# Expert tiles of a gated cross-attention network: rows as two planes of 16-bit halves, fetched by transposing transfers

## What is computed

```python
diff = x[:, :, None, :] - keys
dist2 = jnp.sum(diff * diff, axis=-1)
logits = -dist2 + jnp.einsum('bld,ed->ble', x, rw) + rb
topv, topi = jax.lax.top_k(logits, TOP_K)
w = jax.nn.softmax(topv, axis=-1)
hidden = jax.nn.gelu(jnp.einsum('bld,efd->blef', x, w1) + b1, approximate=False)
exp_out = jnp.einsum('blef,edf->bled', hidden, w2) + b2
sel = jnp.take_along_axis(exp_out, topi[..., None], axis=2)
fused = jnp.sum(w[..., None] * sel, axis=2)
```

## Time and profile before

| | |
|---|---|
| median of 3 runs | 1582.33 us (1581.99 to 1583.48) |
| the profiled execution | 1586.09 us, of which the profile's span is 1584.2 us |
| mean granted clock of PE | 0.963 |
| dispatch beside A3 | about 853 to 1255 us of the span |
| expert loop | 1263 to 1548 us, 144 tiles |
| loading back, mixing, storing | 1549 to 1584 us |
| PE busy | 87% of the span |

### The profile page before, as it was taken

One profiled execution on the slowest core, in us unless ns is written; L12 is line 12 of the kernel. 1 busy time (PEld: TensorE's weight loads), 2 busy tenths in 40 slices (PEclk: granted clock), 3 DMA queues, 4 the chain that ended last, 5 costly groups with the idle time before them and its releaser, 6 DMA issues.

```text
span 1584.2 us, 34370 instructions
## 1 busy us (share of the span) xinstructions
PE 1383.6 (87%) x9959; PEld 1030.9 (65%) x9982; DVE 1103.3 (70%) x3531; ACT 1014.4 (64%) x2931; POOL 534.7 (34%) x631
## 2 busy tenths in 40 slices
PE   4788887998899988998999999999986299999994
PEld 3566665676744465443666666666665199999994
DVE  4788877687777667883666876776665466666665
ACT  2688887554555564225788777777764377777762
POOL 3353467222211411010003242242144455555550
PEclk9999999999999999999999999999987599999998
DMA  8000059500499910000000010010034122222227
GB/s 195 24 8 7 14 84 177 80 0 14 91 177 176 149 34 21 1 0 7 1 8 25 12 34 23 13 35 16 23 125 160 40 65 62 66 65 65 62 57 265
DMA packets 143406, 98.23 MB, mean 62 GB/s; under 512 B 20595, under 2 KB 132510, under 8 KB 142150
## 3 DMA queue, kind: packets, MB, share of 16 engines
q1 hardware_dynamic: 134598, 80.08, 25.4%
q0 software_dynamic: 8704, 16.87, 3.2%
HBM read 43.03 MB, written 54.93 MB: 62 GB/s over the span
## 4 chain that ended last, share of the span: by engine, by line
PE 59%; ACT 13%; DVE 12%; issue 10%; DMA 2%; another core or an unknown queue 1%; SPq 1%; DVEq 1%; POOL 0%; ACTq 0%; POOLq 0%
PE bank L1448 7%; PE bank L1006 7%; PE bank L1440 7%; PE bank L1292 4%; PE bank L1022 4%; ACT arena L1481 4%; PE bank L947 3%; PE bank L1057 3%; ACT att L1618 3%; PE bank L1010 2%; PE bank L1042 2%; PE bank L1032 2%; ACT att L1483 2%; PE bank L929 2%; PE bank L1368 2%
## 5 line engine op out<-in xcount | busy, mean ns | idle before, releaser
L1481 ACT ACTIVATE arena<-bank 128x512 f32<-128x512 f32 (+7 forms) x380 | 245.5, 674 | 151.4 <-PE bank L1355 54.1
L1898 ACT ACTIVATE att<-bank,arena 128x128 f32<-128x128 f32 x576 | 164.5, 371 | 67.5 <-PE bank L1440 64.6
L820 POOL DMA_INDIRECT expert_outputs<-arena x144 | 146.9, 1020 | 146.3 <-issue 99.5
L1618 ACT ACTIVATE att<-bank,arena 128x128 f32<-128x128 f32 x512 | 180.2, 393 | 16.1 <-DVE arena L2156 15.0
L774 POOL DMA_INDIRECT dispatched_rows<-arena x112 | 113.4, 1012 | 177.1 <-DVE arena L2045 116.1
L608 POOL TENSOR_TENSOR ve<-mv,eps 128x4 f32<-128x4 f32 x64 | 12.8, 200 | 423.9 <-DVE mv L1961 414.9
L1448 PE MATMUL bank<-arena,att 128*128 128x128 f32 x1152 | 153.7, 276 | 2.3 <-ACT att L1898 1.1
L1440 PE MATMUL bank<-xnT,arena 128*128 128x128 f32 x1152 | 153.8, 277 | 0.9 <-ACT xnT L1481 0.9
L1448 PEld LDWEIGHTS bank<-arena,att 128*128 128x128 f32 x1152 | 140.1, 192 | 4.8 <-ACT att L1898 4.6
L1440 PEld LDWEIGHTS bank<-xnT,arena 128*128 128x128 f32 x1152 | 141.4, 193 | 1.5 <-ACT xnT L1481 1.5
L1481 ACT ACTIVATE xnT<-bank 128x128 f32<-128x128 f32 (+1 forms) x180 | 63.4, 352 | 90.1 <-PE bank L841 42.4
(11 more groups left out here) (375 smaller groups left out, 3243.6 us busy)
## 6 DMA issues: line engine op xcount, KB each, us to landing
dispatched_rows<-padf SPq DMA_DIRECT2D x16, 2128.5 KB, 32.7
arena<-dispatched_rows SPq DMA_DIRECT2D x144, 64.5 KB
cxT<-in_ctx SPq DMA_DIRECT2D x32, 256.0 KB
arena<-in_L_ffn_w SPq DMA_DIRECT2D x8, 1024.0 KB
arena<-expert_outputs SPq DMA_DIRECT2D x8, 1024.0 KB, 14.3
expert_outputs<-arena POOLq DMA_INDIRECT x144
out_x<-x SPq DMA_DIRECT2D x8, 256.0 KB, 4.2
dispatched_rows<-arena POOLq DMA_INDIRECT x112
```

The lines of the kernel that those rows point to most:

```text
L820: pl.indirect_dma_start(sent_out, bass.IndirectOffsetOnAxis(xtu3[:, s, P:P + 1], 0), yt3[:, s, :], None, bounds_check=TOP3 * TOKENS - 1, o ...
L1481: copy = lambda o, i: nc.scalar.activation(o, i, ACT.Copy)
L1618: last = nc.scalar.activation(ex3_of(w, side)[:, i, :], bank[side][:, i * P:i * P + P], ACT.Exp, bias=nm3[:, w % 2, h:h + 1], accum_out=su ...
L1898: last = nc.scalar.activation(h3[:, s % 2, k * P:k * P + P], bank[s % 2][:, k * P:k * P + P], ACT.Gelu, bias=b1c3[:, s % 4, k:k + 1])
```

## The change

Rows go out as two planes of 16 bits: all 128 low halves of a row's words, then all 128 high halves, then the tag's word. A row keeps its 516 bytes.

- In dispatch ACT's row copy becomes two (`row_halves`), each of as many elements as the one before, but of 16 bits, reading every second half-word. The second, u = 11, stands one step later, ahead of the exponential u = 10.
- In the loop SP fetches a tile by one transposing transfer (128 rows x 256 half-words into 128 partitions x two planes) and one small transfer of the 128 tags (4 bytes each). It reads the places of four tiles at once, in the loop ahead of the wait for the scatter.
- PE's `tile_T` is gone. ACT's copy from PSUM becomes `tile_join`: it waits for the group's transfers, reads the two planes from SBUF and writes low and high half of each word side by side into `xnT`, 256 half-words per partition, in the place in ACT's order where the copy stood.
- POOL takes the tags from a tile of their own.

```diff
-            def load_tile(i, s):
-                at = sp.value_load(tab3[0:1, 1, bass.ds(i, 1)], min_val=0, max_val=UNUSED)
-                sp.dma_start(xt3[:, s, :], sent[bass.ds(at, P), :]).then_inc(sem(f"F3_tiles_loaded{s // GROUP3}"), 16)
-
-            for s in range(SLOTS3):
-                load_tile(s, s)
+            def places_of(i):
+
+                _, places = nc.values_load_multi_w_load_instructions(tab3[0:1, 1, bass.ds(i, GROUP3)], [mybir.EngineType.SP], min_val=0, max_val=UNUSED)
+                return places
+
+            def load_tile(at, s):
+                sp.dma_start_transpose(xth3[:, s, :, :], sent[bass.ds(at, P), 0:HALF_WORDS3]).then_inc(sem(f"F3_tiles_loaded{s // GROUP3}"), 16)
+                sp.dma_start(tagh3[:, s, :], sent[bass.ds(at, P), HALF_WORDS3:2 * ROW3]).then_inc(sem(f"F3_tiles_loaded{s // GROUP3}"), 16)
+
+            for q in range(SLOTS3 // GROUP3):
+                places = places_of(q * GROUP3)
+                for k in range(GROUP3):
+                    load_tile(places[k], q * GROUP3 + k)
             with sp.Fori(1, GROUPS3) as g:
-                for s in range(SLOTS3):
-                    if s % GROUP3 == 0:
-
-                        sp.wait_ge(sem(f"F3_scattered{s // GROUP3}"), g * (16 * GROUP3))
-                    load_tile(g * SLOTS3 + s, s)
+                for q in range(SLOTS3 // GROUP3):
+                    places = places_of(g * SLOTS3 + q * GROUP3)
+                    sp.wait_ge(sem(f"F3_scattered{q}"), g * (16 * GROUP3))
+                    for k in range(GROUP3):
+                        load_tile(places[k], q * GROUP3 + k)
...
-            def tile_T(turn, s):
-                pe.wait_ge(sem(f"F3_tiles_loaded{s % SLOTS3 // GROUP3}"), turn * (16 * GROUP3) + 16 * GROUP3)
-                nc.tensor.transpose(bank[6 + s % 2][:, 0:P], xt3[:, s % SLOTS3, 0:P], ident[:, :]).then_inc(sem("F3_tile_T"), 1)
...
             with pe.Fori(0, GROUPS3 - 1) as g:
                 for s in range(SLOTS3):
-                    tile_T(g + (s + 2) // SLOTS3, s + 2)
                     up(g * SLOTS3 + (s + 1), s + 1)
                     down(g * SLOTS3 + s, s)
...
+            def row_halves(half, h):
+
+                js = ALL if half is None else HALVES[half]
+                n, of = len(js), slice(js[0], js[-1] + 1)
+                return copy(rows_of(half)[0][:, qs_of(js), h * P:h * P + P].rearrange("p (j k) d -> p j k d", j=n),
+                            xrh3[:, of, :, h].unsqueeze(2).to_broadcast([P, n, TOP3, P]))
...
-                    copy(rows_of(half)[0][:, qs_of(js), 0:P].rearrange("p (j k) d -> p j k d", j=n),
-                         xr3[:, of, :].unsqueeze(2).to_broadcast([P, n, TOP3, P])).then_inc(sem("F3_rows_copied"), 1)
+                    row_halves(half, 0)
+                if u == 11:
+                    row_halves(half, 1).then_inc(sem("F3_rows_copied"), 1)
...
-                        if live and not first and more and w in (3, 5, 6):
-                            routing(c - 1, {3: 8, 5: 9, 6: 10}[w])
+                        if live and not first and more:
+                            for u in {3: (8,), 5: (9,), 6: (11, 10)}.get(w, ()):
+                                routing(c - 1, u)
...
-            def tile_T(n, s):
-                act.wait_ge(sem("F3_tile_T"), n + 1)
-                copy(xnT[:, (s % 4) * P:(s % 4) * P + P], bank[6 + s % 2][:, 0:P]).then_inc(sem("F3_tile_xT"), 1)
+            def tile_join(n, turn, s):
+                act.wait_ge(sem(f"F3_tiles_loaded{s % SLOTS3 // GROUP3}"), turn * (32 * GROUP3) + 32 * GROUP3)
+                copy(xnh[:, s % 4, :, :], xth3[:, s % SLOTS3, :, :].rearrange("p h t -> p t h")).then_inc(sem("F3_tile_xT"), 1)
```

More of the change, by code:

```diff
@@ L8 @@
 U32 = mybir.dt.uint32
+U16 = mybir.dt.uint16
 I32 = mybir.dt.int32
@@ L45 @@
 ROW3 = P + 1
+HALF_WORDS3 = 2 * P
 UNUSED = E3 * REGION
@@ L220, in flamingo @@
         padu3 = padf3[:, :].bitcast(U32)
+        padh3 = padf3[:, :].bitcast(U16)
         iota3 = sb("iota3", [E3, NT])
@@ L346, in flamingo @@
         rowsu3 = arena[:, used[0] - SC * ROW3:used[0]].bitcast(U32).rearrange("p (q d) -> p q d", q=SC)
+        rowsh3 = arena[:, used[0] - SC * ROW3:used[0]].bitcast(U16).rearrange("p (q d) -> p q d", q=SC)
         lg3 = ar([P, CB, E3])
@@ L357, in flamingo @@
         xr3 = tmp2
+        xrh3 = tmp2[:, :, :].rearrange("p j d -> p (j d)").bitcast(U16).rearrange("p (j d h) -> p j d h", j=CB, h=2)
+        xnh = xnT[:, :].bitcast(U16).rearrange("p (s t h) -> p s t h", s=4, h=2)
         xrT3 = we2[:, 0:W]
@@ L369, in flamingo @@
         tabf3, tab3 = ar([1, 2, NT]), ar([1, 2, NT], I32)
+        at = used[0] = -(-used[0] // 8) * 8
+        xt3 = ar([P, SLOTS3, P])
+        xth3 = arena[:, at:used[0]].bitcast(U16).rearrange("p (s h t) -> p s h t", s=SLOTS3, h=2)
         at = used[0]
-        xt3 = ar([P, SLOTS3, ROW3])
-        xtu3 = arena[:, at:used[0]].bitcast(U32).rearrange("p (s d) -> p s d", s=SLOTS3)
+        tag3 = ar([P, SLOTS3])
+        tagu3, tagh3 = arena[:, at:used[0]].bitcast(U32), arena[:, at:used[0]].bitcast(U16).rearrange("p (s h) -> p s h", s=SLOTS3)
         yt3 = ar([P, SLOTS3, P])
@@ L390, in rows_of @@
         def rows_of(half):
-            return (rows3, rowsu3, di3) if half is None else (last3, lastu3, lastdi3)
+            return (rowsh3, rowsu3, di3) if half is None else (lasth3, lastu3, lastdi3)
         def qs_of(js):
@@ L402, in diagonal @@
             return (flat_wv3 if q < SC // 2 else flat_wo3)[:, q % (SC // 2), :]
-        sent = nc.dram_tensor("dispatched_rows", (UNUSED + P, ROW3), F32, kind="Internal").ap()
+        sent = nc.dram_tensor("dispatched_rows", (UNUSED + P, 2 * ROW3), U16, kind="Internal").ap()
         sent_out = nc.dram_tensor("expert_outputs", (TOP3 * TOKENS, P), F32, kind="Internal").ap()
@@ L520, in _ @@
                 if st == "A1":
-                    sp.dma_start(sent[UNUSED:UNUSED + P, :], padf3[:, :]).then_inc(sem("F3_prefilled"), 16)
+                    sp.dma_start(sent[UNUSED:UNUSED + P, :], padh3).then_inc(sem("F3_prefilled"), 16)
                     prefill(range(PREFILLED_F0))
@@ L1450, in down @@
                 last.then_inc(sem("F3_down"), 1)
-            tile_T(0, 0)
-            tile_T(0, 1)
             up(0, 0)
@@ L1636, in body @@
                             piece(c + 1, 1 - p, s)
-                        if live and not first and more and w in (3, 5, 6):
-                            routing(c - 1, {3: 8, 5: 9, 6: 10}[w])
+                        if live and not first and more:
+                            for u in {3: (8,), 5: (9,), 6: (11, 10)}.get(w, ()):
+                                routing(c - 1, u)
                         if live and not more:
-                            for u in {3: (8,), 5: (9, 10)}.get(w, ()):
+                            for u in {3: (8,), 4: (9,), 5: (11, 10)}.get(w, ()):
                                 routing(c - 1, u)
                         if not live:
-                            for u in {0: (8,), 1: (9,), 2: (10,)}[w]:
+                            for u in {0: (8,), 1: (9,), 2: (11, 10)}[w]:
                                 routing(c - 1, u, 0)
@@ L1875, in _ @@
             stage_start(act, STAGE["F3"])
-            for u in (8, 9, 10):
+            for u in (8, 9, 11, 10):
                 routing(NC, u, 1)
@@ L1900, in up @@
                 last.then_inc(sem("F3_gelu"), 1)
-            tile_T(0, 0)
-            tile_T(1, 1)
+            tile_join(0, 0, 0)
+            tile_join(1, 0, 1)
             with act.Fori(0, GROUPS3 - 1) as g:
@@ L1906, in _ @@
                     up(g * SLOTS3 + s, s)
-                    tile_T(g * SLOTS3 + (s + 2), s + 2)
+                    tile_join(g * SLOTS3 + (s + 2), g + (s + 2) // SLOTS3, s + 2)
             for s in range(SLOTS3):
@@ L1911, in _ @@
                 if n + 2 < NT:
-                    tile_T(n + 2, s + 2)
+                    tile_join(n + 2, GROUPS3 - 1, s + 2)
             for i in range(2, len(MIXED3)):
```

7 lines of the change are left out of this document (3 added, 4 removed).

## The result

The changed kernel takes 1666.75 us (median of four runs, 1661.44 to 1667.99) against 1582.90 us for the one before: a ratio of 1.0522, interval 1.0508 to 1.0537. It is slower, and outside the range given. It is the case that the prediction had as its first rival, at the value of that rival's high end (1667), though not by that rival's own arithmetic.

The account below looks back on a forecast made before the run. PE was taken to pace the expert loop at 1.90 us a tile. Terms -15.4 + 1.9 + 3 + 0 = -10.5 us, from the median 1582.33 us, gave 1571.8 us; range 1565 to 1640 us.

Parts of the forecast that it names:

- first rival: Expert loop: SyncE's queue or the engines behind it need over 1.3 us a tile; 1667 us at high end; chance 0.28.
- (a): Expert loop: PE's transpose goes, 0.107 us for each of 144 tiles, -15.4 us.
- (b): Expert loop: the PSUM copy becomes a 0.42 us join, covered except at the turn's table load; +1.9 us (0 to 3.3).
- rival that ScalarE eats the gain: Expert loop: a join takes 0.84 us, a turn 23.8 us instead of 23.1; 1593 us; chance 0.15, shared with A3.
- the one that PE does not move: Expert loop: `up` starts stay 1.90 us apart because weight loading, not the transpose, made the 0.11 us; 1587 us; chance 0.04.
- (c): A3 in dispatch: a second row copy per chunk makes `values` late by 0.5 us, six chunks; +3 us (0 to 12).
- (d): Expert loop: two transfers per tile take SyncE 0.68 us (high bound 2.2), hidden with 2.6 us to spare.
- (e): First fill before the loop: four places, four pairs and landing, not hidden; -1.4 to +1.9 us, taken as 0.
- the ring's allowance: Expert loop: time from a group's scatter to its slots' first use, 10.13 us without the turn's loss, taken as 5.3 tiles.
- break-even: Expert loop: at 1.47 us of SyncE per tile today's pace of 1.90 us is reached; from there the kernel is slower.
- The ring: Expert loop: reloading the ring of slots by transposing transfers becomes the bound; 1613 us at 1.7 us a tile; chance 0.28.

Follow-up runs that it names:

- after: The changed kernel, with all parts of the change, against the kernel before it: 1666.75 us, ratio 1.0522.
- before: The kernel without the change, which the changed kernel is compared with: 1582.90 us.

## Why the prediction was wrong, by its own steps

- **(a) PE's transpose goes, -15.4 us.** Right. Removed alone, with the turn's loss of (b), it was to give -13.5 us and gave -11 (interval -8 to -14). In after, `up`s in a group start 1.78 us apart.
- **(b) The join.** Right, a little low: 0.42 us was forecast, and the row says 0.458:

```profile
L1489 ACT ACTIVATE xnT<-arena 128x256 uint16<-128x256 uint16 x144 | 65.8, 458 | 114.4 <-DMA arena<-dispatched_rows 110.2
```

  The 16-bit halves cost what other elements do (bounds were 0.29 and 0.84). With plain transfers the turn is 22.1 us, forecast 21.9, and ScalarE still waits 0.32 us for each `up`. The rival that ScalarE eats the gain is out (its price of 1593 comes to 1594 by its own terms), and so is the one that PE does not move.
- **(c) Two row copies, +3 us.** Right as far as it can be told: +2.8 (interval 1.0 to 4.6), with copies that are slower than those of the change.
- **(a) to (c) together** are the run with plain transfers: -6 us, forecast -10.5. Of the 4.4 missing some 1.1 are the first fill, and 2.5 lie in (a) and (b), by the run without PE's transposes; the rest is within the intervals. A few stalls as at 1375 above, which no step had, are in both runs.
- **(d) Two transfers a tile.** This is the step that failed. It took 2 x 0.34 = 0.68 us of SyncE for a tile and the places as hidden. Measured: the transposing one 1.37 with its gap, the tags 0.55, the places 0.50. The pair alone, 1.92, lies near the upper of its two bounds (0.68 and 2.2); with the places the queue needs 2.42 us a tile, beyond both, where PE needs 1.79. Three choices were wrong in it. First, 0.34 is what the instruction's row shows, not what it takes of the queue: plain pairs in the first fill start 0.52 us apart, and one transfer with its gap is 0.55. Second, the nearest row for an unknown form was taken as its value, when no row showed the form at all. Third, the places were called hidden because they now stand ahead of the wait; they are hidden only as long as SyncE has to wait there, and in after it never does. The same condition decides the experiments on before: there four places at once change nothing.
- **(e) The first fill.** Forecast 0 (-1.4 to +1.9), measured +4.3. Four places and four pairs are 2.0 + 4 x 1.93 = 9.7 us, not 3.5 to 5.8; it is the same wrong term. Landing behind the last issue took 1.2 us (1269.5 to the join at 1270.68), less than the 1.5 to 2.5 assumed.
- **The rival's price.** It named the mechanism and the signs that then showed: joins waiting for DMA on every fourth tile, SyncE never waiting. That its price was 1667 is luck, two errors that cancel. Its r was 2.2 where 2.45 is right. And it kept the ring's allowance, scatter to first use, at 5.3 tiles for any pace. That is 9 tiles, from the last of a group to the first of the same slots in the next turn, less the lag of a scatter behind its tile, which is a time: 9 x 1.90 + 0.28 - 10.41 = 7.0 us. The ring then asks for 9 tiles >= 4.2 + 7.0 + 4r, a tile of (11.2 + 4r)/9: 2.22 us at r = 2.2, some 1634 us, and 2.33 at r = 2.45. Above r = 2.24 the queue's own r is the larger, so at 2.45 the queue sets the pace and SyncE never waits, as the trace shows. Near the break-even the two formulas agree (1.47 and 1.47), so the threshold was right and the slope too steep.
- **The chances.** The ring had 0.28 and the range ended at 1640. The forecast leaned on an unknown price taken at the low end of bounds that lay a factor of three apart, with the break-even (1.47) in their middle. The rows given against the upper half, 0.34 us an issue and idle DMA engines, were all of plain transfers.

The Trainium skill (VectorE: DVE Perf Modes, "The three transpose paths") gives 1309 ns for one 128x128 transpose of 16-bit elements by a transposing DMA. One plane took 1.11 us of the queue here, which is near it, though the page does not say what its time counts. Two planes in one instruction took 1.19 us of the queue, not the 2.6 that the prediction made of the figure by doubling it. The Trainium skill (Advanced Engine Details and Errata, "X-Bar Transpose (TRN2)") has transposing DMAs as fast as regular ones. The DMA engines' share, 0.24 after and 0.23 before, does not contradict that; for the queue's time it does not hold here, 1.19 us against 0.33.

## What to carry to other kernels

Before work is moved from an engine to a queue, write out the queue's time for one unit of the loop, with the gaps between its instructions and with register readings and their checks, and compare it with the loop's pace: here 1.92 us of two transfers and 0.50 of a place stood against 1.79. A transfer form that no row shows has no price; measure it alone first, or give the upper bound as much weight as the lower. A step off PE is worth only its start-to-start time (0.11 us here), however long its row looks.

## What the runs showed of the hardware

- A transposing transfer of 128 rows held SyncE's queue 1.19 us with 256 16-bit values a row and 1.11 us with 128, while a plain one of the same rows held it 0.33 us. The DMA engines were busy about a quarter of the time with either (0.24 with two planes transposed, 0.27 with plain transfers).
- Reading values from a tile into registers took 0.27 us for one, 0.87 for four and 2.40 for twelve; the range check of each value was another 0.23 us (37 us less without the 144 of them).
- After some of its pauses of about 2 us PE ran at a granted clock of 0.5, the 1.2 GHz level. In after, nine of its waits in the loop were followed by this. The length alone did not decide: a wait of 2.85 us before 1480.35 was not followed by it, one of 2.03 us before 1588.45 was. The windows around the wait before 1410.97:

```profile
1408.00:1410.00 2.00, 0.87 (x8) 0.68 (x7) 1.42 (x6) 0.00 (x0) 0.99 (x1) 1.00 0.38 91
1410.00:1412.00 2.00, 1.03 (x5) 1.03 (x6) 0.75 (x4) 1.53 (x6) 1.01 (x1) 0.80 0.13 41
1412.00:1414.00 2.00, 2.00 (x12) 2.00 (x11) 0.00 (x0) 1.38 (x6) 0.00 (x0) 0.50 0.16 33
```

  It costs nothing there, as PE then has to wait for the next group anyway; in the run with tags once and no range check, where PE paces, it does.
- At some places PE's signals came 1.3 to 3.6 us late and in a bunch, for instance three of them between 1375.37 and 1375.56 and three between 1508.04 and 1508.22, each time for three sets whose starts were spread over 1.8 us. The engines that waited for PE stood still until then. The cause is open.
